# Records and row gathers issued in groups behind their landings, head sums by a ones column, and reordered layer borders in an eight-layer GNN/FFN kernel

## The reference

```python
x = x + L0_gnn(norm(x))   # per head: softmax over a dense 384x384 score table, then @ v, then elu
x = x + L0_ffn(norm(x))   # six experts, top 2
x = x + L1_gnn(norm(x))   # four blocks: modulated norm, sparse attention as dense masks, MLP
x = x + L1_ffn(norm(x))   # 16 experts of 96 places, top 2: rows scattered to places, results gathered
x = x + L2_gnn(norm(x))   # edge scores, softmax per destination node, out[dst] += alpha * h[src]
x = x + L2_ffn(norm(x))   # eight experts, all mixed
x = x + L3_gnn(norm(x))   # four heads of 512
x = x + L3_ffn(norm(x))   # mean over the nodes -> router -> one of three attention variants
```

## Time and profile before

| | us |
|---|---|
| three timed runs | 1850.32, 1850.44, 1849.62 (median 1850.32) |
| the profiled execution, its own time | 1841.83 |
| its span, first to last instruction | 1840.1 |
| PE busy | 1601.8 (87%), granted clock 0.925 on the mean |
| DVE, POOL, ACT busy | 886.2, 645.1, 501.0 |

### The profile page before, as it was taken

How to read it: one execution, slowest core, us unless ns; L and a number is a source line. 1 busy time by engine, 2 the same in 40 slices (tenths; PEclk the granted TensorE clock), 3 DMA queues, 4 the chain that set the end, 5 groups by cost and what they waited for, 6 DMA issues and landing times.

```text
span 1840.1 us, 22730 instructions
## 1 busy us (share of the span) xinstructions
PE 1601.8 (87%) x6886; PEld 886.1 (48%) x6916; DVE 886.2 (48%) x2166; ACT 501.0 (27%) x1608; POOL 645.1 (35%) x756
## 2 busy tenths in 40 slices
PE   5989999997798999996995976488699899999698
PEld 3534444446454555463553745333244455555455
DVE  8878888887624524432353154576632101011322
ACT  1134444446422324141231214211110211111233
POOL 5867787862322335453002613457300000000000
PEclk9999999998698999997997886589899999999899
DMA  7021101007223132321216734346315122211020
GB/s 305 12 96 24 58 24 59 24 12 202 40 91 117 51 100 53 88 76 33 92 46 134 277 97 143 99 126 178 125 56 202 69 74 68 97 47 34 6 63 17
DMA packets 119547, 161.71 MB, mean 88 GB/s; under 512 B 49433, under 2 KB 61657, under 8 KB 119090
## 3 DMA queue, kind: packets, MB, share of 16 engines
q1 hardware_dynamic: 93024, 115.43, 20.2%
q0 software_dynamic: 18592, 29.91, 6.0%
q10 hardware_dynamic: 7858, 15.44, 2.5%
HBM read 145.26 MB, written 15.47 MB: 87 GB/s over the span
## 4 chain that ended last, share of the span: by engine, by line
PE 78%; DVE 12%; another core or an unknown queue 3%; issue 3%; ACT 2%; DMA 1%; POOL 0%; DVEq 0%; ACTq 0%; POOLq 0%
PE psum L373 76%; DVE stats L464 1%; DVE arena L2622 1%; DVE ring L1281 1%; PE psum L1012 1%; DVE xn L2042 1%; DVE xn L2048 0%; PE psum L2248 0%; DVE xn L2061 0%; DVE ring L656 0%; DVE mv L465 0%; PE psum L398 0%; DMA x<-in_x 0%; POOL tab_x L2291 0%
## 5 line engine op out<-in xcount | busy, mean ns | idle before, releaser
L373 PE MATMUL psum<-arena 128*128 128x128 f32 (+9 forms) x1814 | 328.9, 338 | 57.9 <-issue 31.7
L373 PE MATMUL psum<-arena,ring 128*128 (+1 forms) x1478 | 322.8, 363 | 9.0 <-issue 6.2
L373 PE MATMUL psum<-xT,ring 128*128 128x384 f32 x928 | 321.2, 508 | 9.8 <-ACT ring L3068 4.2
L373 PEld LDWEIGHTS psum<-arena 128*128 128x128 f32 (+5 forms) x1814 | 201.0, 157 | 191.7 <-issue 117.2
L373 PE MATMUL psum<-ring,arena 128*128 128x512 f32 (+1 forms) x592 | 273.4, 610 | 14.0 <-issue 6.6
L373 PE MATMUL psum<-ring,xT 128*128 128x512 f32 x552 | 250.5, 606 | 4.0 <-DMA bc<-in_wide 2.9
L373 PEld LDWEIGHTS psum<-xT,ring 128*128 128x128 f32 x928 | 183.2, 199 | 141.4 <-issue 31.4
L373 PEld LDWEIGHTS psum<-arena,ring 128*128 128x128 bf16 (+1 forms) x1504 | 139.2, 115 | 130.0 <-issue 28.6
L373 PEld LDWEIGHTS psum<-ring,arena 128*128 128x128 f32 (+1 forms) x592 | 103.4, 189 | 140.8 <-issue 139.4
L1063 ACT ACTIVATE ring<-ring 128x128 f32<-128x128 f32 x416 | 123.3, 297 | 173.1 <-DVE ring L1347 168.6
L373 PEld LDWEIGHTS psum<-ring,xT 128*128 128x128 f32 x552 | 104.3, 194 | 125.3 <-issue 119.9
(11 more groups left out here) (468 smaller groups left out, 1632.6 us busy)
## 6 DMA issues: line engine op xcount, KB each, us to landing
ring<-in_L_ffn_w SPq DMA_DIRECT2D x22, 1024.0 KB, 6.6
ring<-in_L_gnn_m_w SPq DMA_DIRECT2D x8, 1024.0 KB
ring<-in_L_ffn_expert_weights SPq DMA_DIRECT2D x8, 1024.0 KB
ring<-tab_key ACTq DMA_DIRECT2D x24, 256.0 KB
ring<-in_L_gnn_Wv SPq DMA_DIRECT2D x5, 1024.0 KB, 5.2
tab_w<-xn SPq DMA_DIRECT2D x6, 768.0 KB, 14.6
ring<-in_L_gnn_Ww SPq DMA_DIRECT2D x4, 1024.0 KB, 7.7
ring<-in_L_gnn_wq SPq DMA_DIRECT2D x4, 1024.0 KB, 5.8
```

The source lines that it names most:

```text
L373: return nc.tensor.matmul(o, a, b, start=start, stop=stop)
```

## The change

- Records: POOL waits before every second scatter, for both scatters of the pair before. Within a pair it waits for nothing.
- Row gathers: 39 buffers (eight more, in `xT`, `xT2` and `xn2`). For the first 39 gathers, POOL waits before every sixth for all that were issued; between them the old wait for the gather four before stays. From gather 39 on, the old rule stands. Row semaphores are eight instead of 31.
- Layer 0: exp without accumulator; the value matrix gets a 65th column of ones per head, and the sum comes out of the product; DVE takes the reciprocal when it scales the head. The node totals' product goes between the second and the third value product, and DVE's largest score of tile three goes ahead of the wait for them. SP waits until both halves of the last score tile have landed, before it issues further loads.
- L1_ffn: three loads for the first group, PE transposes by row tile; ACT copies the last five expert results out itself; DVE does the fold for the next layer (`l2_fold`) and `l2_prologue` in one piece.
- L2_gnn: ACT takes the roots of tiles 1 and 2 before it turns blocks 1 and 2.
- L3_ffn: the router's means by 12 small PE products with a column of ones and one DVE sum; ACT copies two chunks, does the router's relu, then the other two.
- Output: one store per row tile, each when its PSUM bank has been drained.

```diff
-GR = 31
+GR = 39
@@ rows, L2_gnn
+        ROW_GROUP = 6
         def row_landed(eng, T):
-            earlier = 1 if T % GR < 2 * NT else RECORDS + ST // UN if T % GR >= GR - UN else 0
-            eng.wait_ge(rows_landed[T % GR], 16 * (earlier + T // GR + 1))
+            earlier = 1 if T % UN < 2 * NT else 0
+            eng.wait_ge(rows_landed[T % UN], 16 * (earlier + T // UN + 1))
...
                 if T >= GR:
                     pool.wait_ge(msg_used, T - GR + 1 + 2 * RB)
-                if T >= ROWS_UNDERWAY:
+                if 0 < T < GR and T % ROW_GROUP == 0:
+                    for k in range(max(T - ROWS_UNDERWAY, 0), T):
+                        row_landed(pool, k)
+                elif T >= ROWS_UNDERWAY:
                     row_landed(pool, T - ROWS_UNDERWAY)
@@ records, POOL
-                few_underway(pool, q, RECORDS, OF_RECORDS)
+                if q >= OF_RECORDS and q % OF_RECORDS == 0:
+                    for k in range(q - OF_RECORDS, q):
+                        pool.wait_ge(ranks_landed[k % UN], 16 * (RECORDS + k // UN + 1))
@@ layer 0: PE, ACT, DVE, SP
             for t in range(NT):
                 pe_rows(pe, f"l0o{t}", xT, w, t, r_bv0)
-            pe.wait_ge(totals_ready, 1)
-            b = banks.open(pe, "totals")
...
+                if t == 1:
+                    pe.wait_ge(totals_ready, 1)
+                    b = banks.open(pe, "totals")
...
-                            last = mm(b[:, t * HD:(t + 1) * HD], pwT[g % 2][:, c, t * P:(t + 1) * P],
-                                      ost[:, c, g * HD:(g + 1) * HD], c == 0, c == NT - 1)
+                            last = mm(b[:, t * (HD + 1):(t + 1) * (HD + 1)], pwT[g % 2][:, c, t * P:(t + 1) * P],
+                                      ost[:, c, g, :], c == 0, c == NT - 1)
...
-                                            bias=gate[:, 5, t * H8 + h:t * H8 + h + 1],
-                                            accum_out=gate[:, 9, h * NT + t:h * NT + t + 1])
+                                            bias=gate[:, 5, t * H8 + h:t * H8 + h + 1])
...
             chunk_max(1)
+            chunk_max_by_halves(2)
             b = banks.filled(dve, "totals")
...
-            chunk_max_by_halves(2)
...
+                od.link(V.reciprocal(s3, b[:, :, HD]))
+                od.link(V.tensor_tensor(s3, s3, keep.rearrange("p (t h) -> p h t", h=H8)[:, h, :], ALU.mult))
...
+            sp.wait_ge(w_loaded[0], 32)
+            sp.wait_ge(w_loaded[NT - 1], 16)
             for g in range(AHEAD_BASES):
                 load_base_rows(sp, g)
@@ L1_ffn: ACT
+            def take_result(e):
+                act.wait_ge(results_stored[e % GE], 16 * (e // GE))
+                b = banks.filled(act, f"f1e{e}")
+                nc.scalar.activation(eo[0:CAP1, e % GE, :], b[0:CAP1, :], ACT.Copy).then_inc(banks.free_of(f"f1e{e}"), 1)
+                store_result(e)
...
-            load_group(0)
+            load_first_group()
@@ L2_gnn: ACT
-            for t in range(NT):
+            act_row_std(act, ROW_L2, 0)
+            act_turned_block(act, "l2x", xT, 0)
+            for t in range(1, NT):
                 act_row_std(act, ROW_L2 + t, t)
+            for t in range(1, NT):
                 act_turned_block(act, "l2x", xT, t)
@@ L3_ffn: PE, DVE
+                for c in range(KC):
+                    last = mm(means[:, c * NT + t:c * NT + t + 1], xn[:, t, c * P:(c + 1) * P], ones[:, 0:1], True, True)
...
+            nc.vector.tensor_reduce(route[:, 0:KC], b, AX, ALU.add).then_inc(banks.free_of("f3m"), 1)
@@ output
-            sp.wait_ge(out_ready, 1)
-            sp.dma_start(tiled(out), x[:]).then_inc(stored, 16)
-            sp.wait_ge(stored, 16)
+            for t in range(NT):
+                banks.drained(sp, f"f3y{t}")
+                sp.dma_start(out[t * P:(t + 1) * P, :], x[:, t, :]).then_inc(stored, 16)
+            sp.wait_ge(stored, 16 * NT)
```

More of the change, by code:

```diff
@@ L609, in gnn_ffn_program @@
         go_rows = [view(k * D, D) for k in range(RB)] + [ring.slot(s_)[:, c, :] for s_ in (5, 6, 7, 0, 4, 3) for c in range(KC)]
+        go_rows += [v.rearrange("p c n -> p (c n)")[:, k * D:(k + 1) * D] for v, ks in ((xT, (0, 1, 2)), (xT2, (0, 2))) for k in ks]
+        go_rows += [xn2[:, t, :] for t in range(NT)]
         assert len(go_rows) == GR
@@ L2153, in gnn_ffn_program @@
         GE = 4
+        ACT_RESULTS = 11
         xrows = view(0, 2 * NT, D)
@@ L2211, in _ @@
                 nc.scalar.activation(hid1[:, e % 2, :], b[:, 0:FC * CAP1], ACT.Relu).then_inc(banks.free_of(f"f1h{e}"), 1)
-                if e >= 2:
+                if 2 <= e < ACT_RESULTS + 2:
                     store_result(e - 2)
-            for e in range(E1 - 2, E1):
-                store_result(e)
+                if e > ACT_RESULTS:
+                    take_result(e - 1)
+            take_result(E1 - 1)
         @on("pe")
@@ L2243, in transposes @@
             def transposes(g):
-                pe.wait_ge(group_in[g % 2], 16 * (g // 2 + 1))
+                if g == 0:
+                    bk = [banks.open(pe, f"f1t0{c}") for c in range(KC)]
+                    for t in range(NT):
+                        pe.wait_ge(first_group[t], 16)
+                        for c in range(KC):
+                            last = nc.tensor.transpose(bk[c][:, t * P:(t + 1) * P], xrows[:, t, c * P:(c + 1) * P], ident[:])
+                            if t == NT - 1:
+                                last.then_inc(banks.full_of(f"f1t0{c}"), 1)
+                    return
+                pe.wait_ge(group_in[g % 2], 16 * (g // 2 if g % 2 == 0 else g // 2 + 1))
                 for c in range(KC):
@@ L2356, in _ @@
                 od.link(V.tensor_tensor(g, g, kept[:, NT * k:NT * k + NT], ALU.mult))
-            for e in range(E1):
+            for e in range(ACT_RESULTS):
                 if e >= GE:
@@ L2362, in _ @@
                 V.tensor_copy(eo[0:CAP1, e % GE, :], b[0:CAP1, :]).then_inc(banks.free_of(f"f1e{e}"), 1)
-                if E1 - GE - 1 <= e < E1 - 1:
-                    l2_fold(dve, od, e - (E1 - GE - 1))
+            for j in range(GE):
+                l2_fold(dve, od, j)
+            banks.filled(dve, f"f1h{E1 - 1}")
             l2_prologue(dve, od)
@@ L2985, in _ @@
         def _(pe, o):
-            pe_transpose_rows(pe, "f3x", xn, 6 * NT)
+            bk = [banks.open(pe, f"f3x{c}") for c in range(KC)]
+            means = banks.open(pe, "f3m")
+            for t in range(NT):
+                pe.wait_ge(row_ready, 6 * NT + t + 1)
+                for c in range(KC):
+                    last = mm(means[:, c * NT + t:c * NT + t + 1], xn[:, t, c * P:(c + 1) * P], ones[:, 0:1], True, True)
+                if t == NT - 1:
+                    last.then_inc(banks.full_of("f3m"), 1)
+                for c in range(KC):
+                    last = nc.tensor.transpose(bk[c][:, t * P:(t + 1) * P], xn[:, t, c * P:(c + 1) * P], ident[:])
+                    if t == NT - 1:
+                        last.then_inc(banks.full_of(f"f3x{c}"), 1)
             rw1 = ring.get(pe, r_slot)
-            for c in range(KC):
-                banks.drained(pe, f"f3x{c}")
+            banks.drained(pe, "f3m")
             b = banks.open(pe, "f3r")
@@ L3017, in values @@
                 last.then_inc(banks.full_of(f"f3o{h}"), 1)
+            for c in range(KC):
+                banks.drained(pe, f"f3x{c}")
             w = ring.slot(q_slot)
@@ L3058, in _ @@
             nc.scalar.activation(gate[:, 15, 40:41], eps_col[:], ACT.Exp)
-            for c in range(KC):
-                b = banks.filled(act, f"f3x{c}")
-                nc.scalar.activation(xT[:, c, :], b[:, 0:N], ACT.Copy, accum_out=route[:, c:c + 1]).then_inc(banks.free_of(f"f3x{c}"), 1)
+            for c in range(KC // 2):
+                act_copy(act, f"f3x{c}", xT[:, c, :], N)
             b = banks.filled(act, "f3r")
             nc.scalar.activation(route[:, 4:5], b[:, 0:1], ACT.Relu, bias=c_rb1, scale=1.0 / N).then_inc(banks.free_of("f3r"), 1)
+            for c in range(KC // 2, KC):
+                act_copy(act, f"f3x{c}", xT[:, c, :], N)
             banks.drained(act, "f3g")
@@ L3127, in _ @@
                 nc.vector.tensor_tensor(x[:, t, :], x[:, t, :], b, ALU.add).then_inc(banks.free_of(f"f3y{t}"), 1)
-            for t in range(NT):
-                banks.drained(dve, f"f3y{t}")
         block = ctx.enter_context(nc.Block())
```

37 lines of the change are left out of this document (20 added, 17 removed).

## The result

Measured beside each other, the changed kernel took 1805.01 us (median of four, 1803.10 to 1806.64), the kernel before 1849.97: a ratio of 0.9765, 95% interval 0.9739 to 0.9791. The forecast was 1812.0, with 1790 to 1836 as its range. The two profiled executions lie 38.7 us apart in their spans, 1840.1 and 1801.4; the sum had said 38.3.

A forecast was written before the change was run, and what follows sets the result against it. PE, busy 87% of the span, was taken as the bound, with two large standstills. Terms summed to -38.3 us: 1841.83 profiled became 1803.5, plus the 8.5 offset to the timed median 1812.0; range 1790 to 1836.

The forecast's parts named there:

- Records, -17.8: L1_gnn: pausing per pair of record scatters makes block 2's first half like block 1's, -17.8 us (0 to 17.8).
- The pair's period: Record stream in L1_gnn: issuing two records plus one landing takes 4.5 us, so the stream ends near 900.
- The cover of 88 us: L1_gnn: the time between the record stream's expected end near 900 and SP's read back at 988.29.
- Sixes, -14: L2_gnn row gathers: pausing every six leaves 15.3 of 29.1 us of remote waits, a gain of 14 (5 to 41).
- the first reading: L2_gnn gathers: standstill starts 3.5 us into each six, losing 5.1 us; gain 3.6 plus 0.7 in the loop.
- I count no cost: L2_gnn: the sixes delay POOL's score parts by 15 us, priced at nothing since DVE and PE run during pauses.
- Layer 0, -2.8: Layer 0: the first exp starts 3.7 us earlier; later reciprocals and 65 columns cost some back; -2.8 us net.
- Output, -0.8: Output: the last 256 KB store takes between 2.7 and 3.5 us, a memset and drain go; -0.8 (0.25 to 1.2).
- The small edits: All parts other than records and gathers, from layer 0 to the output: -6.5 us together.
- (4): Rival: streams are not the cause of the standstills, so only the small edits pay; 1843.8 us, chance 0.07.
- (5): Rival: slow record landings outlast the cover, delaying SP's read back and expert weights; 1854 us, chance 0.05.
- The sign of being wrong: Changed profile: remote waits without a long POOL stream beside them, or SP's read back waiting for records, would refute the forecast.

The follow-up runs named there:

- e1: The kernel before with only the records in pairs: 1822.09 us, ratio 0.9896.
- e5: The changed kernel itself, run again on another chip: 1774.34 us, ratio 0.9988.
- e2: The changed kernel with the row gathers as before (31 buffers, wait for the gather four back): 1815.73 us, ratio 0.9878.
- e9: The kernel before, unchanged, run for its profile on another chip: 1774.54 us.
- e3: The changed kernel with 39 buffers but the old wait for the gather four back: 1819.71 us, ratio 0.9892.

## Why the prediction was right, and where not

- **Records, -17.8.** Measured -20.0 between the two profiles, 71.5 us in place of 89.87 in e1's chain. The mechanism (a stream without a pause starves the others, a pause per pair frees them) holds on the first chip and on chip a. The step that failed is its cause: "their instructions, which come by DMA queues too". The earlier trace rows already spoke against it. In the records events are late, in the scores PE stands by itself, and why either happens stays open. And I took the standstill for a property of the program; it is one of program and chip (or moment). On chip c this term is 0.
- **The pair's period**, 4.5 us, was mis-sized: 5.1. The wait for a landing was 2.97 us on the mean (148.4 us in 50 waits) against the bucket scatters' 2.29, though the traffic beside those was no smaller (86 GB/s from 435 to 665 us of before, 68 from 666 to 850); why is open. The cover of 88 us left 32.
- **Sixes, -14.** Measured -5.8 in the score stage and -6.0 in the loop, 11.8. Near the value, by two errors, which is luck. For the stage the first reading, a gain of 3.6, was nearer: 22.7 us stay in six waits, where I had taken half of 5.1 us per six and 15.3 in all (the 5.1 itself was worked out with 1.1 us behind the last issue, though the text beside it has 1.5). What that reading put at 0.7 in the loop was 6.0, which the fewer and shorter standstills there explain only in part.
- **"I count no cost" for POOL's score parts.** This failed. On chip b DVE waits 6.26 us for the second. On the first chip DVE has no wait for POOL in the stage; I take it that PE was so late by itself that POOL's delay was hidden. The reason that I gave, that DVE and PE run while POOL pauses, says nothing about work that POOL itself does behind the pause.
- **Layer 0, -2.8**: the first exp comes 3.4 us earlier behind the end of the loop over edges (3.7 by forecast; 3.4 in every kernel with this edit), and of it 3.0 are left at the first row sum of L1_gnn, 3.3 on chip c. **First group, 0**: -0.6. **Last expert result, -1.6**: -1.7. **Roots, -1.5**: -1.9, more than the 1.72 us of PE's wait that I had gone by. **Router, +0.2**: -0.5 by the first attention scores behind it. **Output, -0.8**: -1.7, outside its bound of 1.2: a store of 256 KB took 2.0 us, less than the 2.7 of the smaller load that I had as its lower end.
- **The sum.** -20.0 - 5.8 - 6.0 - 3.0 - 0.6 - 1.7 - 1.9 - 0.5 - 1.7 = -41.2, and against it 3.1 us by which layer 0's loop ended late in this execution (in e5, the same kernel, it ended 3.4 us earlier, so it is chance), with a remainder of -0.6, which block 1 gained. The small edits, -6.5 by forecast, come to -6.4 between e1 and e2 by medians, and to -10.0 on chip c, where the records in pairs are worth nothing.
- **The rivals.** (4), that the streams are not the cause, was put at 1843.8 us. By e1 it is wrong on chip a. The rule behind it is that a DMA engine goes round its queues (the Trainium skill, DMA: Bandwidth & Descriptors, on queues, rings and completion order). No run here contradicts it: chip c has the same streams and nobody waits, and what was late in the records was an event between two engines, which is no transfer of a queue in the trace. The rule excluded less than I had made of it. (5) did not come near: its point was a mean wait of 4.0 us, and the mean was 5.1 - 2.2 = 2.9.
- **The sign of being wrong.** "Remote waits stay where no long stream of POOL stands beside them": one does, the 6.75 us behind the loop. It tells nothing against the streams, since e1 shows it as a wait for PE's own work; the sign was badly chosen, because the name remote covers both.

## What to carry to other kernels

A wait called remote, beside a long stream of indirect transfers, is a reason to break the stream; where its landings have time, a pause for every pair cost nothing here and went with a smaller spread (25 us to 10). Ask first whether the engine waited for is itself at work: the name alone doesn't tell. Where the work on the issuing engine has a reader (POOL's scores here), every pause is paid on a chip that never stood still, so such work may belong ahead of the pause (untested here). And a gain read from one profile on one chip needs a second chip before it is called the kernel's.

## What was not expected of the hardware

- The same program took 1775 us on chips b and c and 1848 to 1850 on the first and chip a. The profiles' granted clock on the mean was 0.944 (e9) and 0.925. PE's busy time is the smaller part of the difference: in the changed kernel 1601.7 us on the first chip and 1590.1 on chip b, 11.6 of the 32 us between their spans; in the unchanged one 1601.8 and 1588.6, 13.2 of 67.3.
- Between 818 and 851 us PE worked on for 23 us while DVE heard nothing of it, and its words came up to 18 us late.
- In the scores PE itself slowed down to 19 matmuls in 18 us (e3), while it waited for nothing that the trace shows.
- Eight more buffers with the old rule made the longest standstill, 19.0 us (e3).
